# Differential attention with a ternary feed-forward: the coefficient of two heads at once, a third buffer for the second exponentials, and a later order for differences and turns

## The reference, cut to what matters

```
x = x + attention(layernorm(x))
x = x + W2q gelu(W1q layernorm(x) + b1) + b2          # W1q, W2q ternary, width 2048

attention: 16 heads, each with two score maps of depth 16, keys and values shared by two heads
  p0, p1 = softmax(q0 k0 + causal), softmax(q1 k1 + causal)      # 1024 x 1024 each
  diff   = p0 - lambda * p1
  head   = rmsnorm(diff @ v) * subln_weight * (1 - lambda_init)  # v is 32 wide
  attention = concat(heads) @ Wo
```

## Time and profile before

| | us |
|---|---|
| median of 3 runs | 4360.22 (4357.92 to 4360.78) |
| profiled execution | 4360.82 |
| its span in the trace | 4359.0 |
| PE busy | 3567.8 (82%) |
| DVE busy | 3379.6 (78%) |
| ACT busy | 2885.3 (66%) |
| POOL busy | 1443.7 (33%) |

### The profile page before, as it was taken

One profiled execution on the slowest core, in us unless ns is written; L12 is line 12 of the kernel. 1 busy time (PEld: TensorE's weight loads), 2 busy tenths in 40 slices (PEclk: granted clock), 3 DMA queues, 4 the chain that ended last, 5 costly groups with the idle time before them and its releaser, 6 DMA issues.

```text
span 4359.0 us, 81492 instructions
## 1 busy us (share of the span) xinstructions
PE 3567.8 (82%) x23454; PEld 2128.7 (49%) x23454; DVE 3379.6 (78%) x6194; ACT 2885.3 (66%) x6786; POOL 1443.7 (33%) x1564
## 2 busy tenths in 40 slices
PE   2688888888888888888888888888988888888886
PEld 1355554455445454554545544455544555454553
DVE  6778977888678886788767887778977788678881
ACT  1577766777567775677756766667766777567782
POOL 1233233332332333322343323333133332333323
PEclk7898999999999998999899989999999999999998
DMA  3100011100001001100011000101011000111000
GB/s 128 41 19 28 19 32 33 33 14 28 30 27 33 22 25 33 32 19 28 20 32 33 30 22 23 34 23 32 19 33 32 28 19 19 33 33 32 14 28 12
DMA packets 146817, 128.38 MB, mean 29 GB/s; under 512 B 66608, under 2 KB 117680, under 8 KB 145840
## 3 DMA queue, kind: packets, MB, share of 16 engines
q1 hardware_dynamic: 146352, 122.79, 8.8%
HBM read 67.61 MB, written 55.12 MB: 28 GB/s over the span
## 4 chain that ended last, share of the span: by engine, by line
PE 45%; DVE 20%; issue 18%; ACT 11%; POOL 3%; ACTq 1%; DMA 1%; DVEq 1%; SPq 0%; POOLq 0%
PE M L831 10%; DVE NM L676 7%; PE F L916 7%; PE M L881 7%; PE F L903 6%; PE SP_ L846 6%; PE DP L858 4%; DVE NM L684 3%; ACT HP L607 3%; ACT E L552 2%; PE M L825 2%; ACT DT L564 1%; DVE CC L696 1%; PE SP_ L847 1%; ACT HP L613 1%
## 5 line engine op out<-in xcount | busy, mean ns | idle before, releaser
L552 ACT ACTIVATE E<-SP_,NM 128x256 f32<-128x256 f32 (+7 forms) x2048 | 1522.6, 744 | 965.0 <-DVE NM L684 480.4
L676 DVE TENSOR_REDUCE NM<-SP_ 128x1 f32<-128x896 f32 (+3 forms) x1024 | 1031.7, 1018 | 236.3 <-PE SP_ L847 228.5
L846 PE MATMUL SP_<-KST,QST 96*128 96x512 f16 (+3 forms) x3072 | 860.0, 353 | 355.7 <-ACT E L552 308.4
L699 DVE SCALAR_TENSOR_TENSOR E<-E,CC 128x512 f32<-128x512 f32 (+7 forms) x1024 | 929.9, 908 | 36.2
L858 PE MATMUL DP<-ident,E 128*128 128x128 f32 x3328 | 601.9, 298 | 150.3 <-ACT DT L564 80.7
L564 ACT ACTIVATE DT<-DP 128x512 f32<-128x512 f32 (+3 forms) x1024 | 524.7, 512 | 219.2 <-PE DP L858 200.7
L684 DVE TENSOR_REDUCE NM<-SP_ 128x2 f32<-128x1024 f32 (+3 forms) x512 | 420.1, 820 | 304.5 <-PE SP_ L847 299.3
L846 PEld LDWEIGHTS SP_<-KST,QST 96*128 96x128 f16 x3072 | 285.1, 103 | 694.7 <-ACT E L552 452.3
L903 PE MATMUL F<-X2H,W1Q 128*128 128x256 f16 x2048 | 496.0, 281 | 94.1 <-ACT HP L607 76.2
L858 PEld LDWEIGHTS DP<-ident,E 128*128 128x128 f32 x3328 | 402.0, 152 | 331.8 <-ACT DT L564 148.6
L831 PE MATMUL M<-WQKV,WT 128*128 128x512 f32 x1040 | 544.6, 617 | 6.3 <-DVE T L659 4.3
(11 more groups left out here) (94 smaller groups left out, 4741.2 us busy)
## 6 DMA issues: line engine op xcount, KB each, us to landing
scratch<-SPL SPq DMA_DIRECT2D x65, 576.0 KB, 2.8
QST<-scratch SPq DMA_DIRECT2D x390, 64.0 KB, 2.4
X<-in_x SPq DMA_DIRECT2D x66, 256.0 KB, 2.8
out<-SQ SPq DMA_DIRECT2D x64, 256.0 KB, 2.0
KST<-scratch SPq DMA_DIRECT2D x390, 32.0 KB, 1.9
DT<-in_w2T SPq DMA_DIRECT2D x1, 4096.0 KB, 25.8
KST<-in_w1T SPq DMA_DIRECT2D x2, 1024.0 KB, 11.4
WQKV<-in_wqT SPq DMA_DIRECT2D x1, 1024.0 KB, 6.7
```

Of the source, the lines that this page charges most:

```text
L552: act.activation(dst, score_out(i, 2 * n + k, w), ACT.Exp, bias=NM[:, (2 * u + k) % 8:(2 * u + k) % 8 + 1], scale=1.0, accum_out=SUM[:, i ...
L676: nc.vector.tensor_reduce(NM[:, m:m + 1], score_out(i, 2 * n + k, P * (i + 1)), AX.X, ALU.max, negate=True).then_inc(max_ready, 1)
L699: nc.vector.scalar_tensor_tensor(out=E1[:, u % 4, 0:w], in0=E2[:, u % 2, 0:w], scalar=CC[:, u % 4:u % 4 + 1], in1=E1[:, u % 4, 0:w], op0=A ...
L846: pe.matmul(SP_[:, k[a // 512], 0:n], q, KST[0:ROWS, a // P:(a + n) // P, kk, :], start=True, stop=not last)
```

## The change

- `diff` is split. A new `ratios` makes the reciprocals and coefficients of an even head and the odd head after it: one reciprocal on 128x2, one scalar_tensor_tensor on 128x2 with lambda as its scalar, in place of two reciprocals and two tensor_scalars with two pointer scalars.
- The order on DVE: at even s, h = 1: `ratios` of heads s-2 and s-1, then the difference of s-2; at odd s, h = 0: the difference of s-2. Before: head s-1 at every h = 1. So even heads come two half steps later and odd heads one.
- On PE the turns of an even head come at half step 2n+6 (was 2n+4), of an odd head at 2n+5, at the end of h = 1; `half_v` one half step later. The copies on ACT: for odd s, h = 0: (s-3, group 0); h = 1: (s-3, group 1) and (s-2, group 0); for even s, h = 0: (s-3, group 1). Before: one copy in each half step.
- E2 has three buffers, with the waits of `E2_FREE`.
- Most constants move by one half step; SUM_INVERSE, RMS_ROWS, LN2_ROWS, LN2_TURN, LN2_REST, the first and second product and their GELUs and splits stay.

```diff
+E2_FREE = (-1, 0, -2) + tuple(range(1, N_U - 2))
-LN1_STATS, LN1_ROWS, LN1_TURN = 1, 3, 6
-Q_PROJ, Q_ROPE = (8, 9, 10, 11), 12
-KV_PROJ, KV_ROPE = (13, 14, 15, 15), 16
-Q_TURN, Q_REST, K_TURN, K_REST = 17, 18, 21, 22
+LN1_STATS, LN1_ROWS, LN1_TURN = 1, 3, 7
+Q_PROJ, Q_ROPE = (9, 10, 11, 12), 13
+KV_PROJ, KV_ROPE = (14, 15, 16, 16), 17
+Q_TURN, Q_REST, K_TURN, K_REST = 18, 19, 22, 23
-PV_OUT = (20, 4)
-SUM_INVERSE, AT_TURN, AT_ROWS = 5, 7, 7
-MEAN_SQ, RMS_ROWS, AN_TURN = 10, 14, 23
-O_PROJ, O_SUM = (24, 25, 26, 27), 28
-LN2_STATS, LN2_ROWS, LN2_TURN, LN2_REST = 28, 30, 31, 31
+PV_OUT = (21, 5)
+SUM_INVERSE, AT_TURN, AT_ROWS = 5, 8, 8
+MEAN_SQ, RMS_ROWS, AN_TURN = 11, 14, 24
+O_PROJ, O_SUM = (25, 26, 27, 28), 29
+LN2_STATS, LN2_ROWS, LN2_TURN, LN2_REST = 29, 30, 31, 31
+def turns(s, h):
+    if s % 2 == 0:
+        return [(s - 3, 1)] if h == 0 else []
+    return [(s - 3, 0)] if h == 0 else [(s - 3, 1), (s - 2, 0)]
...
-        E2 = sb("E2", [P, 2, S], F32)
+        E2 = sb("E2", [P, 3, S], F32)
...
-                    old = T.before(s - 2)
                     if T.attend:
                         exp(T, s, h)
-                    if old and (h == 0 or groups(old[1]) == 2):
-                        dt_copy(*old, h)
+                    for n, g in turns(s, h):
+                        old = T.before(n)
+                        if old and g < groups(old[1]):
+                            dt_copy(*old, g)
...
-            def diff(b, i, n):
+            def ratios(b, i, n):
                 u = i * H + n
                 gu = b * N_U + u
+                col = 8 * (n // 8) + (n % 8) // 2
+                c = slice(u % 4, u % 4 + 2)
+                after(dve, exp_done, 2 * gu + 4)
+                nc.vector.reciprocal(R2[:, c], SUM[:, i % 2, 1, col:col + 5:4]).then_inc(d_chain, 1)
+                after(dve, d_chain, gu + 1)
+                nc.vector.scalar_tensor_tensor(out=CC[:, c], in0=SUM[:, i % 2, 0, col:col + 5:4], scalar=neglam[:, 0:1],
+                                               in1=R2[:, c], op0=ALU.mult, op1=ALU.mult).then_inc(d_chain, 1)
+                after(dve, d_chain, gu + 2)
+
+            def diff(b, i, n):
+                u = i * H + n
                 w = P * (i + 1)
-                col = 8 * (n // 8) + 4 * (n % 2) + (n % 8) // 2
-                after(dve, exp_done, 2 * gu + 2)
-                nc.vector.reciprocal(R2[:, u % 4:u % 4 + 1], SUM[:, i % 2, 1, col:col + 1]).then_inc(d_chain, 1)
...
-                    if h == 1 and T.before(s - 1):
-                        diff(*T.before(s - 1))
+                    done = T.before(s - 2)
+                    if done and s % 2 == 0 and h == 1:
+                        ratios(*done)
+                        diff(*done)
+                    if done and s % 2 == 1 and h == 0:
+                        diff(*done)
...
+            def turn_head(T, n):
+                done = T.before(n)
+                if done:
+                    for g in range(groups(done[1])):
+                        diff_transposes(*done, g)
...
                     if h == 0:
-                        if T.before(s - 2):
-                            for g in range(groups(T.before(s - 2)[1])):
-                                diff_transposes(*T.before(s - 2), g)
-                        half_v(T, s - 3, 1)
+                        if s % 2:
+                            turn_head(T, s - 3)
+                        half_v(T, s - 3, 0)
...
                     else:
-                        half_v(T, s - 2, 0)
+                        if s % 2:
+                            turn_head(T, s - 2)
+                        half_v(T, s - 3, 1)
```

More of the change, by code:

```diff
@@ L547, in exp @@
                 else:
-                    after(act, d_ready, b * N_U + u - 1)
-                    dst = E2[:, u % 2, 0:w]
+                    after(act, d_ready, b * N_U + E2_FREE[u])
+                    dst = E2[:, u % 3, 0:w]
                 col = 8 * (n // 8) + 4 * (n % 2) + (n % 8) // 2
@@ L685, in row_max_pair @@
                                         negate=True).then_inc(max_ready, 2)
+            def ratios(b, i, n):
+                u = i * H + n
+                gu = b * N_U + u
+                col = 8 * (n // 8) + (n % 8) // 2
[6 more added lines that the diff above has]
+                after(dve, d_chain, gu + 2)
             def diff(b, i, n):
                 u = i * H + n
-                gu = b * N_U + u
                 w = P * (i + 1)
-                col = 8 * (n // 8) + 4 * (n % 2) + (n % 8) // 2
-                after(dve, exp_done, 2 * gu + 2)
-                nc.vector.reciprocal(R2[:, u % 4:u % 4 + 1], SUM[:, i % 2, 1, col:col + 1]).then_inc(d_chain, 1)
-                after(dve, d_chain, 2 * gu + 1)
-                nc.vector.tensor_scalar(CC[:, u % 4:u % 4 + 1], R2[:, u % 4:u % 4 + 1], SUM[:, i % 2, 0, col:col + 1],
-                                        neglam[:, 0:1], ALU.mult, ALU.mult).then_inc(d_chain, 1)
-                after(dve, d_chain, 2 * gu + 2)
-                nc.vector.scalar_tensor_tensor(out=E1[:, u % 4, 0:w], in0=E2[:, u % 2, 0:w], scalar=CC[:, u % 4:u % 4 + 1],
+                nc.vector.scalar_tensor_tensor(out=E1[:, u % 4, 0:w], in0=E2[:, u % 3, 0:w], scalar=CC[:, u % 4:u % 4 + 1],
                                                in1=E1[:, u % 4, 0:w], op0=ALU.mult, op1=ALU.add).then_inc(d_ready, 1)
```

## The result

The changed kernel takes 4737.3 us (median of 4 runs, 4736.7 to 4739.9), against 4360.5 for the kernel before on the same chip: a ratio of 1.0867 (1.0851 to 1.0884), 377 us slower. The forecast was 4435, with 4300 to 4490 for 8 in 10. The sign was right and the size was a fifth of the real one.

The account below looks back on a forecast made before the run. No single engine bounds the whole: PE and DVE nearly fill tile 6, tile 1 is a chain of waits. Terms sum to +9.7 us a batch, +74.8 over eight (first 2.8 less), giving 4435; 4300 to 4490 for 8 in 10.

Parts of the forecast that it names:

- move with the turns: All tiles: the other shifted constants follow the turns they were placed beside; no cost was entered.
- the ring: Tiles 5 to 7: closed loop through ACT's exponential and copy, PE's turns and scores, and DVE; +0.3, +1.0, +3.0 us.
- The relief: DVE's merged small operations save 0.28 us a head, paying at 12 chain places in a batch: -3.5 us a batch.
- the rival: DVE's relief decides: all 27 chain places pay 0.28 us, 61 us in all, so the kernel gets faster; chance 0.24.
- DVE busy some 280 us lower: Sign to look for on DVE: total busy time falls by some 280 us over 1024 heads.
- The announced idle times: Tile 7, each pair: DVE idle 1 to 2 us before an even head's second maximum, put down to PE's scores.
- In tiles 0 to 4 the ring is below PE's own work for two heads, and I take nothing.: Tiles 0 to 4: the loop over ACT, PE and DVE is shorter than PE's own work; no cost entered.
- The third split: Ends of tiles 1 and 3: POOL's third hidden-row split now precedes `rstd`, adding 2.8 and 3.1 us a batch.
- some 5 us, not 2.6: Sign at tile 1's end: PE's turns (L825) idle some 5 us, not 2.6, with `rstd` behind a third split.
- The other tile ends: Ends of the six other tiles: later output projection and sum x1 cost 0.5 us each, +3.0 us a batch.
- It would gain nothing and lose nothing by it, as the difference right behind it would have waited for the same lock.: DVE's new two-input coefficient can be locked out by POOL through their shared SBUF port, at no net cost.
- The clock rival: PE's longer waits add stretches at its lower 1.2 GHz clock, 64 us more, 4500 in all; chance 0.09.

Follow-up runs that it names:

- e1: Kernel before with all of the changed kernel's schedule constants and nothing else changed; 4524.6 us, ratio 1.0377.
- e2: Changed kernel with DVE's old order and small operations; later turns and copies, constants and third E2 buffer kept; 4683.2 us, ratio 1.0741.
- e4: Kernel before with odd heads' reciprocals and coefficients left out, using the even head's coefficient (output not the reference's); 4307.8 us, ratio 0.9883.
- e3: Changed kernel with the merged reciprocal and coefficient made one by one again, four small operations a pair; 4832.6 us, ratio 1.1084.
- e13: Changed kernel with the odd head's second group of turns moved on PE behind the scores of the second map; 4685.2 us, ratio 1.0744.
- e6: Changed kernel with the third and fourth split of the hidden rows a half step later, putting the third behind `rstd`; 4736.3 us, ratio 1.0863.
- e11: Kernel before with only O_SUM (the sum x1) and LN2_STATS (second layer norm's statistics) one half step later; 4417.6 us, ratio 1.0129.
- e8: Kernel before with the second group of new constants (K_TURN, K_REST, first of PV_OUT, AN_TURN, O_PROJ, O_SUM, LN2_STATS); 4441.2 us, ratio 1.0186.
- e7: Kernel before with the first group of new constants (LN1_TURN, Q_PROJ to Q_REST, AT_TURN, AT_ROWS, MEAN_SQ); 4437.0 us, ratio 1.0177.
- e15: Changed kernel with the first group of constants (LN1_TURN, projections, Q_TURN, Q_REST, AT_TURN, AT_ROWS, MEAN_SQ) set back to old values; 4725.8 us, ratio 1.0837.
- e14: Changed kernel with turns spread to one copy each half step (4640.4 us), plus the odd head's difference a half step later on DVE; 4556.1 us, ratio 1.0448.
- e16: Kernel before with each head's coefficient as scalar_tensor_tensor with two tensor inputs in place of tensor_scalar, nothing moved; 4398.2 us, ratio 1.0089.
- e9: Changed kernel with one ACT copy, the odd head's group 0, moved behind the next exponential; 4783.8 us, ratio 1.0968.
- e12: Kernel before's constants and odd-head places, with merged operations and both differences at h = 1 of even s; 4852.8 us, ratio 1.1127.

## Why the forecast was right or wrong, step by step

Three sums missed, 302 us in all. The constants were priced at 68 us and cost 164 (e1), the turns and copies at 34 and cost 159 (e2), DVE's order and merge at -28 and cost 54 (149 - 95). The steps that failed are those set to nothing: the constants that "move with the turns", the turns outside the ring, and DVE's order outside the ring. One by one:

**The relief (-3.5 a batch, and 0.28 at 27 places as the rival).** The rival's 61 is near e4's 53 us for the old kernel, though not in the tiles that it counted; the forecast's own 28 had left out tiles 5 to 7, of which 6 and 7 gave 4.0 of e4's 6.2 us a batch. Of the operation: 0.22 was taken, and it is 0.22 where nothing hinders it, 0.26 on the mean. "DVE busy some 280 us lower" was a mistake of kind: the 0.55 a pair was a spacing of starts, hand-overs included, and busy time holds only durations, which gave 222 on the two lines (279 + 156 before, 133 + 80 after). In the new order the merge is worth 95 us, more than e4's 53 in the old one; in e3 all four small operations stand together ahead of an even head's difference, which may be why.

**The ring (+4.3 a batch, 34 us).** Right in mechanism, and 52 us by e13. The division was off: tile 6 had 3.8 us where 1.0 was forecast, tile 7 3.1 as forecast (3.0), tile 5 none. The announced idle times are there before the second maximum of five of six even heads in tile 7 (1.24 to 2.73 us, announced as 1 to 2), but PE waits for the copy in few of these pairs, not in each. The claim beside it failed: "In tiles 0 to 4 the ring is below PE's own work for two heads, and I take nothing." True of the ring, wrong of the turns. Bunching and lateness together cost 159 us with DVE unchanged, 49 of them for lateness alone. From e1 to e2 a batch grew by 20.2 us, 13.0 of them outside tiles 6 and 7.

**The third split (2.8 + 3.1 a batch, 44 us).** In the changed kernel it is worth nothing (e6), though PE's wait in tile 1 was 4.73 us as announced ("some 5 us, not 2.6"). A sign came true whose price did not. The forecast charged the whole split, while the statistics that `rstd` needs come later too (1.75 us of it were left), and priced a local wait as if all behind it moved by the same amount. In the old order tiles 1 and 3 did grow by 2.2 and 3.4 us (e11), near the forecast's 2.8 and 3.1; whose doing that is stays open.

**The other tile ends (3.0 a batch for six tiles, 24 us).** Of the right size in the old order: e8 has 4.3 us in these six tiles, and 10.2 in all against the 8.9 of the terms. With the first batch's 2.8 taken off that is 68 us forecast against 81 measured. In e11 PE waits 1.1 to 2.6 us for the normalised rows in each of the six, and that costs next to nothing in time, 1.1 us together. So it isn't the wait that is the price there either.

**"The other shifted constants move with the turns that they were placed beside."** A sentence without a working, and 77 us in the old order (e7), 1.5 to 1.9 us in each of tiles 2, 3, 4, 6 and 7. Beside the late turns the same group costs little (e15, 12). So the sentence can stand only if the turns' own lateness is then charged with the rest, and the forecast charged neither.

**DVE's order.** No term outside the ring, 149 us measured (e3 against e2). The forecast counted DVE's work in two heads and found less of it, and did not lay it out over the half steps: both differences stand between the second maximum of the even head and that of the odd, none in the other half. From the start of the odd head's second maximum to that of the next even head's DVE has two maxima to do, 2 x 1.13 us, while the way over PE takes 1.25 + 1.26 + 0.71 = 3.2 in tile 7 (maximum to exponential, to scores, to the next maximum, all): a hole of nearly 1 us even without the ring. In e13, where the ring is cut, such holes stand in tile 7 (four of 0.28 to 0.84 us). The order cost 3.0 to 5.0 us in each of tiles 3 to 7 and 0.1 in tiles 0 to 2 together. e14 gets 84 us back; but that the holes are what the 149 us are made of isn't shown. From e2 to e3 the maxima wait only 40 us more, DVE's scaling of the attention 122, the last operation of the second layer norm 79 and PE's turns for it 48, and it is the last two that e14 lowers.

**"It would gain nothing and lose nothing by it, as the difference right behind it would have waited for the same lock."** Wrong: e16, +37 us, with one operation changed to a form that is faster by itself. The delay was not only held earlier in place of later: the two-input form adds 56 us of busy time (335.0 against 279.4), and the difference behind it (L699) was not relieved but slowed, 928 ns on the mean against 908. So each can be caught, one after the other. The Trainium skill (SBUF — State Buffer, "SBUF: two separate sides") has the rule for it, a lock for a whole instruction; the 1.03 us of e16 agree with it.

**The clock rival (0.09, 4500).** Partly true. The mean granted clock went from 0.913 to 0.895. With levels of 1.2 and 2.4 GHz, the time at the lower is twice the missing part of the span: 2 x 0.087 x 4359 = 758 us before, 2 x 0.105 x 4736 = 994 after, 236 more. PE's busy time grew by 122 us for the same 23454 matmuls. 236 us at 1.2 GHz hold the work of 118 at 2.4, so by this estimate 118 of the 377 us are the most that the lower clock itself can have cost. PE also stands idle 254 us more. No run here separates the two. Tile 7 alone went from 0.90 to 0.86.

**What stays open.** Why the bunched turns cost some 45 us beyond the ring (97 - 52, both in the new DVE order) and do so in short tiles too; why the first group's 77 us shrink to 12 beside the rest; whether holes at the maxima or late rows of the second layer norm make DVE's order dear; the clock's share. The range failed because only the terms that were named had bounds, and three parts (first group, turns outside the ring, DVE's layout) were set to nothing without any.

## What to carry to other kernels

In a schedule written by hand over several engines, what freeing an operation is worth can be measured by leaving it out, in one run (e4); what the edit makes late has to be priced at every place, the ones "that only move along" first. Lay the moved work out half step by half step, with what stands behind it in each queue: the same work in another order cost more here (149 us) than the whole saving (95). And a named wait is a place, not a price: removing 375 us of one raised the time by 47, and shortening another by 1.6 us in a tile, where it was plainly exposed, left the time alone.

## What the runs showed of the hardware that I had not expected

The lock between DVE and POOL catches an operation on 128x1 as well as one on 128x896: the two-input form took 0.22 us alone, 1.03 beside a POOL operation, and 0.327 on the mean, against 0.273 for a form with one tensor and two pointer scalars, and that cost 37 us in 4360. The granted clock fell with the waiting, but is no measure of it: the runs of e15 have 0.889 and 0.885 at 4715 and 4737 us, those of e9 0.886 at 4784, and e12, the slowest at 4853, has 0.899.
